# Emptying the row buffer of the second expert block: 34 large transfers during attention, or 8 tails once the counts are known

## What is computed

```python
x = x + 0.5 * _L0_ffn_ref(_layernorm(x), gate, w0, w1, wo)
x = x + _L0_attn_ref(_layernorm(x), wq_a, q_a_norm_w, wq_b, wkv_a, kv_a_norm_w, wkv_b, wo)
x = x + 0.5 * _L0_ffn_ref(_layernorm(x), gate, w0, w1, wo)

# the expert block
gate_logits = jnp.einsum('bsd,de->bse', x, gate_kernel)          # 8 experts
top_k_weights, top_k_indices = jax.lax.top_k(gate_logits, 2)      # 2 of them for each token
top_k_weights = jax.nn.softmax(top_k_weights, axis=-1)
combine = jnp.einsum('bsk,bske->bse', top_k_weights, one_hot)
out = jnp.einsum('bse,bsem,emd->bsd', combine, silu(h0) * h1, wo_kernel)
```

## Time and profile before

| quantity | value |
|---|---|
| device time, median of 3 runs | 1092.42 us |
| lowest and highest | 1091.67 and 1094.03 us |
| the profiled execution: its time | 1092.42 us |
| its span | 1090.3 us |
| PE busy | 1019.9 us (94%) |
| DVE, ACT, POOL busy | 725.8, 523.2, 476.4 us |
| HBM written | 51.34 MB |

### The profile page before, as it was taken

One profiled execution on the slowest core, in us unless ns is written; L12 is line 12 of the kernel. 1 busy time (PEld: TensorE's weight loads), 2 busy tenths in 40 slices (PEclk: granted clock), 3 DMA queues, 4 the chain that ended last, 5 costly groups with the idle time before them and its releaser, 6 DMA issues.

```text
span 1090.3 us, 22650 instructions
## 1 busy us (share of the span) xinstructions
PE 1019.9 (94%) x6232; PEld 806.4 (74%) x6233; DVE 725.8 (67%) x1649; ACT 523.2 (48%) x1139; POOL 476.4 (44%) x417
## 2 busy tenths in 40 slices
PE   4569999999879999999999999999999889999995
PEld 4547888888557777777777777777688658888884
DVE  6364766655487788777887788887556745666542
ACT  1343443432157676766766677766501314443321
POOL 2652344343344653647454744443125513444432
PEclk9999999999999999999999999999999999999998
DMA  9943554532100223213232223232576535644330
GB/s 237 292 166 69 129 127 101 115 52 40 59 0 12 78 79 98 79 44 94 79 98 78 65 74 98 79 98 78 175 232 211 187 110 113 162 104 104 55 57 8
DMA packets 88414, 112.77 MB, mean 103 GB/s; under 512 B 10032, under 2 KB 65456, under 8 KB 88112
## 3 DMA queue, kind: packets, MB, share of 16 engines
q1 hardware_dynamic: 74032, 94.95, 29.4%
q0 software_dynamic: 14304, 16.87, 9.2%
HBM read 64.37 MB, written 51.34 MB: 106 GB/s over the span
## 4 chain that ended last, share of the span: by engine, by line
PE 70%; DMA 13%; issue 6%; DVE 4%; POOL 3%; ACT 1%; POOLq 1%; SPq 0%; DVEq 0%; ACTq 0%
PE bank L1728 11%; PE bank L1755 11%; DMA out<-shared,small 8%; PE bank L1716 5%; PE bank L1717 5%; PE bank L1718 5%; PE bank L1827 4%; DMA x_after_moe<-shared,small 4%; PE bank L1529 4%; PE bank L1531 4%; PE bank L1533 4%; POOL rows_by_expert L560 3%; PE bank L1541 2%; PE bank L1703 2%; PE bank L1704 2%
## 5 line engine op out<-in xcount | busy, mean ns | idle before, releaser
L886 ACT ACTIVATE shared<-bank,small 128x512 f32<-128x512 f32 x256 | 176.3, 689 | 90.1 <-DVE small L1342 89.2
L1342 DVE TENSOR_REDUCE small<-bank 128x1 f32<-128x512 f32 x256 | 174.4, 684 | 40.7 <-PE bank L1718 40.5
L822 ACT CAST split_rows_and_inner<-bank 128x512 fp32r<-128x512 f32 x78 | 45.8, 587 | 237.8 <-PE bank L1514 237.8
L1728 PE MATMUL bank<-constants,shared 128*128 128x128 f32 x1024 | 155.7, 274 | 2.3 <-ACT shared L886 0.7
L1728 PEld LDWEIGHTS bank<-constants,shared 128*128 128x128 f32 x1024 | 121.9, 140 | 44.6 <-issue 13.7
L1531 PE MATMUL bank<-expert_weights_low,split_rows_and_inner 128*128 x312 | 144.0, 462 | 0.0
L1533 PE MATMUL bank<-expert_weights_high,split_rows_and_inner 128*128 x312 | 142.7, 457 | 0.0
L1529 PE MATMUL bank<-expert_weights_high,split_rows_and_inner 128*128 x312 | 125.1, 401 | 2.7 <-DVE split_rows_and_inner L1127 2.5
L1716 PE MATMUL bank<-expert_weights_high,shared_split 128*128 128x512 f32 x256 | 122.3, 478 | 3.6 <-DVE shared_split L1410 2.3
L1132 DVE TENSOR_TENSOR split_rows_and_inner<-bank,split_rows_and_inner 128x512 fp32r<-128x512 f32 x78 | 53.9, 691 | 106.7 <-ACT split_rows_and_inner L822 106.5
L616 POOL TENSOR_TENSOR shared<-shared 128x512 f32<-128x512 f32 x32 | 41.2, 1287 | 187.0 <-DVE shared L1352 179.7
(11 more groups left out here) (197 smaller groups left out, 2192.4 us busy)
## 6 DMA issues: line engine op xcount, KB each, us to landing
rows_by_expert<-empty_rows SPq DMA_DIRECT2D x34, 516.0 KB, 5.4
expert_weights<-L_ffn_w_kernel SPq DMA_DIRECT2D x32, 512.0 KB, 5.2
shared<-rows_by_expert SPq DMA_DIRECT2D x78, 129.0 KB, 2.1
expert_weights<-L_ffn_wo_kernel SPq DMA_DIRECT2D x16, 512.0 KB, 6.3
shared<-inverse_sums SPq DMA_DIRECT2D x64, 128.0 KB, 3.0
attended_transposed<-shared SPq DMA_DIRECT2D x32, 256.0 KB, 5.2
expert_weights<-attended_transposed SPq DMA_DIRECT2D x2, 2048.0 KB, 11.1
shared<-attended_transposed SPq DMA_DIRECT2D x2, 2048.0 KB, 11.0
```

Of the source, the lines that this page charges most:

```text
L886: nc.scalar.activation(prob[k % 4], bank[k % 4][:, :], ACT.Exp, bias=negmax[:, k % 8:k % 8 + 1], accum_out=psum[par][:, hh * GT + qt:hh * ...
L1342: V.tensor_reduce(negmax[:, k % 8:k % 8 + 1], bank[k % 4][:, :], AX.X, ALU.max, negate=True).then_inc(max_ready, 1)
L1728: last = tr(bank[4 + k % 2][:, c * P:(c + 1) * P], prob[k % 4][:, c * P:(c + 1) * P], ident)
```

## The change

The 34 transfers, their constant and POOL's wait for them are taken out. The second block does what the first does: SP and, new, ACT read the counts once they are there and write `zrow` behind each expert's rows, SP for experts 0 to 3 and ACT for experts 4 to 7. SP then waits for all 8 tails before it loads rows.

```diff
-EMPTY = 4
...
                 sp.wait_ge(tables_ready[f], 1)
-                if f == 0:
-                    for e in range(E):
-                        n = sp.value_load(cnt_i[0:1, e:e + 1], min_val=0, max_val=T)
-                        sp.dma_start(xs[bass.ds(n + e * REGION, P), :], zrow[:, :]).then_inc(tails_zeroed[0], 16)
-                    sp.wait_ge(tails_zeroed[0], 16 * (E + SPARE))
+                for e in range(E // 2 if f else E):
+                    n = sp.value_load(cnt_i[0:1, e:e + 1], min_val=0, max_val=T)
+                    sp.dma_start(xs[bass.ds(n + e * REGION, P), :], zrow[:, :]).then_inc(tails_zeroed[f], 16)
+                sp.wait_ge(tails_zeroed[f], 16 * (E if f else E + SPARE))
...
-            def empty_rows(c):
-
-                n = EMPTY * P
-                sp.dma_start(xs[c * n:(c + 1) * n, :].rearrange("(p k) c -> p k c", k=EMPTY),
-                             zrow[:, :].unsqueeze(1).to_broadcast([P, EMPTY, ROW])).then_inc(tails_zeroed[1], 16)
-
...
                 spread(p + 2, p % 2)
-                empty_rows(p)
-                if p % 4 == 0 and p > 0:
-                    empty_rows(NPAIR - 4 + p // 4 - 1)
...
-            pool.wait_ge(tails_zeroed[1], 16 * (E * REGION // (EMPTY * P)))
...
                 split_high(1, 1, piece)
+            act.wait_ge(tables_ready[1], 1)
+            for e in range(E // 2, E):
+                n = act.value_load(cnt_i[0:1, e:e + 1], min_val=0, max_val=T)
+                nc.scalar.dma_start(xs[bass.ds(n + e * REGION, P), :], zrow[:, :]).then_inc(tails_zeroed[1], 16)
             moe(1)
```

## The result

The changed kernel takes 1101.01 us (median of 9 runs, 1097.34 to 1107.50). The kernel before, run beside it, takes 1094.03 us (median of 9, 1091.67 to 1096.16). The ratio is 1.0069, with a 95% interval from 1.0044 to 1.0095: slower by 0.7%, where no difference was forecast. The forecast of 1092.6 us is 8.4 us too low, and the time lies 6 us above the range. The ratios here are taken over all the runs of a comparison; they are not the quotients of the two medians, which would be 1.0064 here.

The account below looks back on a forecast made before the run. TensorE was taken to bound the kernel, with the last scatter gating the second expert block. Attention 0, SP and ACT tails 0 and scatter 0.2 us, added to 1092.42 us, gave 1092.6 us; range 1090.8 to 1095.0.

Parts of the forecast that it names:

- part 1: Attention: taking out the 34 transfers changes nothing, 0 us, with bounds from -1.7 to 1.7 us.
- The rival that the relief would show as a gain: Attention's end and projection: 17.5 MB less DMA makes it faster by 2.3 us, 1090.1 us; chance 0.06.
- part 2: Second seam: SP's four tails, 1.23 us apart, land at 877.4, 0.8 us before the last scatter; cost 0.
- the 0.8 us of room: Second seam: SP's last tail was to land at 877.4, SP being let go by the scatter at 878.2.
- part 3: Second seam: ACT's four tails go at SP's quick pace and land at 877.4; cost 0.
- the upper end: Second seam: with 1.40 us for every ACT issue, the last tail lands at 881.7, 3.5 us late.
- The rule of the Trainium skill: Second seam: SP and ACT share one descriptor generator, 0.33 us more per issue, 0.5 us late; left out of the sum.
- part 4: Second seam: the tails' packets delay the last scatter by 0.2 us, between 0 and 0.7 us.
- The slow stretch of TensorE: Behind the second seam: a longer gap lengthens the stretch of slow matmuls, 0.6 us more, within the slower rival.
- the slower rival: Second seam: late tails on ACT or SP hold SP, 4.1 us in all, 1096.5 us; chance 0.15.
- the gate: Second seam: 878.2, when the last scatter lets SP go; a tail that lands later is paid in full.

Follow-up runs that it names:

- e3_after: The changed kernel without an edit, measured a third time against the kernel before: 1097.77 us against 1098.58 us, ratio 1.0005.
- e3_both_thin: e1_both with each late tail writing only the last two words of its rows, 1 KB in place of 129 KB: 1099.03 us, ratio 1.0011.
- e2_tails_elsewhere: e1_both with the tails written to a buffer that nothing reads, SP waiting for them only at the block's very end: 1100.00 us, ratio 1.0003.
- e1_both: The kernel before with its 34 transfers kept and the 8 tails added, 4 from SP and 4 from ACT, all waited for: 1108.91 us, ratio 1.0028.
- e4_after: The changed kernel without an edit, measured a fourth time against the kernel before, on one more chip: 1100.85 us against 1098.00 us, ratio 1.0032.
- e1_after_again: The changed kernel without an edit, measured a second time against the kernel before: 1110.41 us against 1106.25 us, ratio 1.0050.
- the first profile: The profiled execution of the unedited changed kernel from its first measurement: 1111.73 us, with a span of 1109.5 us.
- the four comparisons: The unedited changed kernel measured against the kernel before on four occasions: ratios 1.0069, 1.0050, 1.0005 and 1.0032.
- e3_act_dynamic: The changed kernel with one more ACT transfer ahead of its wait for counts, 129 KB at a register address, to an unread buffer: 1100.50 us, single run.
- the first comparison: The unedited changed kernel's first measurement against the kernel before: 1101.01 us against 1094.03 us, ratio 1.0069.
- the third: The third comparison of the unedited changed kernel with the kernel before: 1097.77 us against 1098.58 us, ratio 1.0005.
- e3_before: The kernel before without an edit, profiled on the same chip as e3_after: one run of 1092.40 us.

## Why the prediction was wrong

**Attention (part 1) was right.** 34 empties less, and the pairs take 453.0 us from first to last mark, 452.9 to 453.1 us in all 15 profiles, with the empties and without. The comparison within the trace of before was as good as an experiment. The rival that the relief would show as a gain falls.

**The tails on SP (part 2)** came at about the forecast pace: 886.0, 887.5, 889.0 and 890.5, steps of 1.5 us where 1.23 were expected (1.4 in `e3_after`). Their landing was taken as 2.1 us; it is 2.3 to 3.6 in `e3_after`. At 3.6 us the 0.8 us of room in front of the scatter would be gone by this alone, but SP was held by ACT's tails and not by these.

**The tails on ACT (part 3)** fell between the two ends. The first issue takes 2.1 to 2.5 us in all the kernels with a tail on ACT and no transfer like it before, where the sum had 0.34 and the upper end 1.40 for each. In `e3_after` it takes 2.21, 1.9 us more than the sum had, and the landing of 3.8 us in place of 2.1 is 1.7 more. In `e3_after` the last tail lands at 879.5, 10.6 us behind the counts (868.7 + 0.22), against 7.1 in the sum and 11.4 at the upper end. The bounds held; the value taken between them, a cost of 0, didn't. In all four profiles of the changed kernel the last of these tails lands 10.5 to 10.8 us behind the counts, where SP was let go at 7.9 before. So this step failed too, and would have held SP for most of the measured time even with the scatters on time; no run has late tails beside punctual scatters. I had chosen the lower end because SP's row was nearest, and it didn't hold for ACT: SP's own first transfer with an address from a register, at 60.6 in the trace of before, took 0.36 us, and its slow one is the fourth.

The rule of the Trainium skill that was weighed there ("Perfetto Trace Analysis", "DMA Instruction — HWDGE (DVE, Sync)") didn't show as a cost of each issue: SP's and ACT's go in the same microseconds, SP's take 0.33 to 0.38 us and three of ACT's four 0.34.

**The scatters (part 4) are the main step that failed.** The sum had 0.2 us, worked out from occupancy: 12 transfers of 0.35 us in 5 us, "that fits, but with little room", and 0.7 us at the worst. Measured in the four profiles of the changed kernel, SP's wait for the scatters ends 4.6 to 5.5 us after the last one's issue in place of 2.6 to 2.7: 1.9 to 2.8 us late. `e3_both_thin` shows that the written bytes make the delay, and `e2_tails_elsewhere` that nobody has to wait for the tails for it. Two things were wrong in the term. The 0.35 us were read where one queue was writing. Beside the others a transfer takes more of the engines: in the row of `e1_both` SP's four tails take 0.43 us each and ACT's 0.51. And the 5 us were taken as evenly filled, while ACT's late tails pile up on SP's and the scatters and fill the engines to 95% for 2.5 us. That makes the last scatter's last packet 1.1 to 2.5 us late. The rest, 0.1 to 1.3 us, lies between the last packet and the report, for which the sum had nothing beyond a quiet stretch; its reason stays open.

**The slow stretch of TensorE** adds what the slower rival said, in the mean: the transposes come 2.4 us later behind the last scatter (8.2 to 8.6 us in place of 5.9 to 6.1), the outer layer 2.9. Half a us, where 0.6 was forecast for it. By profile it follows the time at the lower clock that lies behind the first transpose: at 4.8 and 5.0 us of it (`e4_after`, `e1_after_again`) from transpose to outer layer is as long as before, within 0.2 us; at 6.6 (`e3_after`) it is 0.8 us longer and at 8.0 (the first profile) 1.3. That even half a us came out is partly luck.

**The rival that came true** is the slower one: right in place, in sign and nearly in size (4.1 us forecast, 2.9 in the profiles, 4.3 in the mean of the four comparisons). Its mechanism, tails of ACT that land late and hold SP, was there: plainly in `e4_after`, by 0.9 us, and by 0.1 us in the others. But its cause, ACT's issues, is only a part; the scatters were late as well, and `e3_act_dynamic` has the delay without the slow issue. It was given 0.15 because the gate, 0.8 us away, was measured against a landing taken from a quiet stretch. The 7.5 us of the first comparison (0.69% of 1094) are more than the seam's 2.9; the rest didn't come back in the third and is not explained.

**The range** also leant on three runs of before, 1091.67 to 1094.03 us. The same kernel later had runs from 1089 to 1114 us. Of a kernel whose expert blocks take from 199.3 to 206.0 us in these profiles from first transpose to last add, three runs tell little.

## What to carry to other kernels

When a wait ends the path, what counts is completion, and a transfer beside others must be priced by how full the engines are in the very microseconds before it ends, not by a mean and not with a landing time read in a quiet stretch. With one other queue writing, the last packet of the scatter wasn't late here; with two it was, by 1.1 to 2.5 us. When two waits end within 0.2 us, the one that the profile names isn't the only cause: look at both. Writes of bulk that nobody is short of time for belong where nothing waits. Here 18 MB in attention cost nothing that a trace shows, and 1 MB at the seam costs 2.9 us. A row read on one engine can price another one badly: the first transfer with an address from a register takes ACT 2.1 to 2.5 us to issue and SP 0.36. And the distances between marks, over several profiles, resolve what medians of runs can't.

## What the runs showed that was not expected

- The first transfer with an address from a register takes 2.1 to 2.5 us to issue on ACT, the next 0.34. One at a fixed address ahead of it (0.36 us) doesn't help; one with a register does. On SP the first such transfer takes 0.36 us, and why the two differ stays open.
- The DMA engines were 63% busy over 10 us in `e1_both` and 95% over 2.5 us in `e3_after`, and beside others ACT's writes of 129 KB still took 3.4 to 4.1 us to land in `e3_after`, and the last scatter 5.6 us in `e3_act_dynamic`, where it is 2.7 in `e3_before`.
- 18 MB of writes fewer in attention leave its 453.0 us from first to last mark as they are, within 0.1 us.
- The granted clock at the second seam is 0.50 for 3.4 us in all four profiles of before, and for 6.8 to 10.2 us in the four of the changed kernel. TensorE stood idle ahead of the transpose for 0.4 to 1.4 us in the former and for 3.6 to 5.7 us in the latter; with 2.8 us in `e3_both_thin` it is 6.8 us too.
- The same kernel on the same chip: a median of 1106.25 us, and 1098.00 us some time later.
